# A ring of three weight halves, and edge rows gathered plainly and summed by VectorE

## The reference

```python
feat = jnp.concatenate([n_f[edge_src], n_f[edge_dst]], axis=1)
e_oo = jax.nn.relu(feat[E_HH:E_HH + E_OO] @ W_oo + b_oo)
logit = (e_f @ W_a + b_a)[:, 0]
m = jax.lax.stop_gradient(jax.ops.segment_max(logit, edge_dst, num_segments=N))
ex = jnp.exp(logit - m[edge_dst])
alpha = ex / den[edge_dst]
z_f = jax.ops.segment_sum(alpha[:, None] * n_f[edge_src], edge_dst, num_segments=N)
h_new = jax.nn.relu(nf2[:NH] @ W_hn + b_hn)
```

## Time and profile before

| | |
|---|---|
| median of three runs | 787.23 us (786.36 to 787.28) |
| the profiled execution | 785.15 us, its span 783.4 us |
| PE busy | 660.7 us (84% of the span) |
| DVE busy | 505.2 us (64%) |
| POOL busy | 259.7 us (33%) |
| ACT busy | 209.5 us (27%) |
| DMA packets of the gathers' queue | 20160, 73.41 MB, 36.1% of 16 engines' span |
| DMA packets of SP's queue | 20800, 88.88 MB, 30.1% |

### The profile page before, as it was taken

How to read it: one execution, slowest core, us unless ns; L and a number is a source line. 1 busy time by engine, 2 the same in 40 slices (tenths; PEclk the granted TensorE clock), 3 DMA queues, 4 the chain that set the end, 5 groups by cost and what they waited for, 6 DMA issues and landing times. The chain is left out here.

```text
span 783.4 us, 8227 instructions
## 1 busy us (share of the span) xinstructions
PE 660.7 (84%) x2739; PEld 467.8 (60%) x2741; DVE 505.2 (64%) x1084; ACT 209.5 (27%) x266; POOL 259.7 (33%) x191
## 2 busy tenths in 40 slices
PE   4999999999847997798999699999955676798952
PEld 3778887788735775575778456677710011586621
DVE  8968813635645556365764597865568896327996
ACT  4333322220332354041614425152220100311001
POOL 3000306655654206247475555401223000002340
PEclk9999999999988999798999999999995779899985
DMA  9753449999999768969999999945360023140201
GB/s 347 257 203 135 141 184 298 296 323 320 323 303 317 269 200 226 306 200 312 306 287 296 317 318 236 303 151 189 108 242 0 0 80 135 54 140 5 108 27 80
DMA packets 41721, 163.40 MB, mean 209 GB/s; under 512 B 5168, under 2 KB 5552, under 8 KB 34512
## 3 DMA queue, kind: packets, MB, share of 16 engines
q0 software_dynamic: 20160, 73.41, 36.1%
q1 hardware_dynamic: 20800, 88.88, 30.1%
q10 hardware_dynamic: 720, 0.59, 0.2%
HBM read 146.08 MB, written 16.78 MB: 208 GB/s over the span
## 5 line engine op out<-in xcount | busy, mean ns | idle before, releaser
L1384 PE MATMUL bank_low<-w_hi,xT_hi 128*128 128x512 f32 x496 | 201.7, 407 | 8.2 <-DVE w_lo L861 3.2
L1385 PE MATMUL bank_low<-w_lo,xT_hi 128*128 128x512 f32 x496 | 196.4, 396 | 0.0
L1386 PE MATMUL bank_low<-w_hi,xT_lo 128*128 128x512 f32 x496 | 196.2, 396 | 0.0
L560 POOL DMA_INDIRECT gathered_rows<-edge_tables,dst_row x68 | 115.8, 1703 | 76.8 <-DMA gathered_rows<-edge_tables,src_row 65.5
L1029 DVE SCALAR_TENSOR_TENSOR gathered_rows<-gathered_rows,wa_bc 128x1024 f32<-128x1024 f32 x68 | 83.0, 1221 | 83.1 <-DMA gathered_rows<-edge_tables,dst_row 83.1
L560 POOL DMA_INDIRECT gathered_rows<-edge_tables,src_row x68 | 87.0, 1279 | 127.2 <-DVE gathered_rows L1029 91.8
L861 DVE TENSOR_TENSOR w_lo<-w_raw,w_hi 128x2048 fp32r<-128x2048 f32 x48 | 107.9, 2288 | 31.2 <-ACT w_hi L633 30.9
L1384 PEld LDWEIGHTS bank_low<-w_hi,xT_hi 128*128 128x128 f32 x496 | 95.3, 192 | 38.0 <-issue 12.3
L1386 PEld LDWEIGHTS bank_low<-w_hi,xT_lo 128*128 128x128 f32 x496 | 95.0, 191 | 20.6
L1385 PEld LDWEIGHTS bank_low<-w_lo,xT_hi 128*128 128x128 f32 x496 | 95.2, 192 | 18.7
L633 ACT ACTIVATE w_hi<-w_raw 128x2048 fp32r<-128x2048 f32 x50 | 92.8, 1902 | 8.3 <-DMA w_raw<-in_wt 8.3
(11 more groups left out here) (269 smaller groups left out, 951.7 us busy)
## 6 DMA issues: line engine op xcount, KB each, us to landing
w_raw<-in_wt SPq DMA_DIRECT2D x54, 1024.0 KB, 8.2
edge_tables<-stage SPq DMA_DIRECT2D x32, 256.0 KB, 7.1
x_in<-in_x SPq DMA_DIRECT2D x4, 512.0 KB, 9.1
xn_scratch<-xn SPq DMA_DIRECT2D x4, 512.0 KB, 4.6
node_top<-stage SPq DMA_DIRECT2D x8, 256.0 KB, 7.7
x_part<-in_x SPq DMA_DIRECT2D x8, 256.0 KB, 5.5
mix_out<-stage SPq DMA_DIRECT2D x8, 256.0 KB, 2.0
xn_raw<-xn_scratch SPq DMA_DIRECT2D x4, 512.0 KB, 5.8
```

The costliest lines, as they stand in the source:

```text
L560: pool.indirect_dma_start(rows_sum[:, s, :], None, table_d[0:rows, :], bass.IndirectOffsetOnAxis(ap=index[:, t:t + 1].bitcast(U32), axis=0 ...
L1384: pe.matmul(dest, lh, rh, start=start and i == 0, stop=False)
L1385: pe.matmul(dest, lh, rl, start=False, stop=False)
L1386: last = pe.matmul(dest, ll, rh, start=False, stop=last_one)
```

## The change

- **Ring.** `w_hi` and `w_lo` hold three halves each instead of two chunks. PE goes through the first half for all row blocks, then through the second, with one bank per row block. A new semaphore `first_halves` tells ACT that a chunk's first half has been read, upon which the second half of the next chunk is copied. SP, ACT and DVE take halves one at a time (`load_next`, `hi_half`, `lo_half`). The very last half, BON1's second, has a place of its own.
- **Edge rows.** With the space that this frees there are five src and five dst buffers in place of six slots. Both gathers of a tile are plain and are issued one behind the other. DVE adds the two (L1052, 128x1024) before the dot. That is 68 more DVE instructions.
- **Order.** Tiles no longer come in pairs: `TILES` says how many stand behind a chunk's first and second half on DVE, and a tile's maximum is taken one tile later. The k and q sums stand in one row behind the chunk's tiles. `ATTEND`, `DEN8` and `KV_AT` move PE's small products to other places. All 36 maxima stand in PR1.

The diff, cut to its core:

```diff
-PAIRS = {4: 2, 5: 3, 6: 2, 7: 3, HHT0: 1, HHT1: 1, K0: 3, V0: 3, HN1: 1, K1: 3, V1: 3, Q0: 2, Q1: 3, ON0: 3, ON1: 1}
-assert sum(PAIRS.values()) * 2 == T_GATHERED
-MAXIMA = {PR0: (0, 18), PR1: (18, 36)}
+RING = 3
+TILES = {5: (3, 2), 6: (3, 2), 7: (3, 2), HHT0: (1, 2), HHB0: (1, 1), HHT1: (1, 2), HHB1: (1, 1),
+         K0: (3, 2), HN0: (1, 1), V0: (2, 3), HN1: (0, 1), K1: (2, 3), V1: (2, 3), Q0: (2, 3), Q1: (2, 3),
+         ON0: (2, 2), ON1: (2, 2), PR0: (2, 0)}
+assert sum(map(sum, TILES.values())) == T_GATHERED
+MAXIMA = {PR1: (0, 36)}
 T_EARLY = 36
-SLOTS = 6
+SLOTS = 5
+LAG = 2
+SECOND = 5
 LOADED = 4
+ADDED_HERE = list(range(T_GATHERED))
...
-USES = [("k", a, j) for a in range(2) for j in range(4)] + [("q", 0, j) for j in range(4)] + \
-       [("q", 1, 0), ("q", 1, 1), ("q", 1, 2), ("z", 0, 0), ("z", 0, 1), ("q", 1, 3), ("z", 0, 2), ("z", 0, 3)] + \
-       [("z", 1, j) for j in range(4)]
-
-ATTEND = {(Q1, 2): [(0, 0), (0, 1)], (Q1, 3): [(0, 2), (0, 3)], (ON0, 2): [(1, 0), (1, 1)], (ON1, 0): [(1, 2)], (ON1, 1): [(1, 3)]}
-DEN8 = {(Q1, 0): 0, (ON0, 0): 1}
+USES = [("k", a, j) for a in range(2) for j in range(4)] + [("q", 0, j) for j in range(4)] + [("z", 0, j) for j in range(4)] + \
+       [("q", 1, j) for j in range(4)] + [("z", 1, j) for j in range(4)]
+
+ATTEND = {(Q1, 1, 0): [(0, 0), (0, 1)], (Q1, 1, 1): [(0, 2), (0, 3)], (ON0, 1, 0): [(1, 0), (1, 1)], (ON0, 1, 2): [(1, 2), (1, 3)]}
+DEN8 = {(Q1, 0, 2): 0, (ON0, 0, 1): 1}
+KV_AT = {(HN1, 0, 0): 0, (Q0, 0, 0): 1}
...
+    w_hi = sb("w_hi", [P, RING, HALF], F32R, at_w_hi)
     bhn1 = sb("bhn1", [P, 2, HALF], F32, at_w_hi)
-    w_lo = sb("w_lo", [P, 2, KT * CW], F32R)
+    w_lo = sb("w_lo", [P, RING, HALF], F32R)
...
+        def load_next(c, h):
+            sp.wait_ge(w_lo_done, 2 * (c - 1) + h + 1)
+            load_half(c, h)
+            if h == 0 and c in BIASED:
+                sp.wait_ge(bias_lo_done, bias_no(c))
+                load_bias(bias_no(c))
+
         for c in range(TABLES):
-            for h in range(2):
-                sp.wait_ge(w_lo_done, 2 * (c + 1) + h + 1)
-                load_half(c + 2, h)
-            if c + 2 in BIASED:
-                sp.wait_ge(bias_lo_done, bias_no(c + 2))
-                load_bias(bias_no(c + 2))
+            load_next(c + 2, 0)
             for m in range(MT):
                 store(4 * c + m + 1, m % 2, table_tiles[c // 2, m, :, (c % 2) * CW:(c % 2 + 1) * CW])
+            load_next(c + 2, 1)
...
+                s = t % SLOTS
                 if t >= SLOTS:
                     pool.wait_ge(edge_dot, t + 1 - SLOTS)
-                gather(t, src_row, src_landed)
-            if t >= LAG:
-                u = t - LAG
-                pool.wait_ge(src_landed[u % SLOTS], 16 * (u // SLOTS + 1))
-                gather(u, dst_row, dst_added, ALU.add)
+                gather(t, rows[:, s, :], src_row, src_landed[s])
+                if t in ADDED_HERE:
+                    n = ADDED_HERE.index(t)
+                    if n >= SECOND:
+                        pool.wait_ge(row_added_here, n + 1 - SECOND)
+                    gather(t, dst_rows[:, n % SECOND, :], dst_row, dst_landed[s])
...
+        def hi_half(c, h):
+
+            if h == 0:
+                act.wait_ge(prod_ready, FIRST[c - 1] + HEAD)
+                if c in BIASED:
+                    n = bias_no(c)
+                    act.wait_ge(bias_loaded, n * 32 + 32)
+                    act.activation(b_hl[0:64, n % 2, :], b_raw[0:64, :], ACT.Copy).then_inc(bias_hi_done, 1)
+            elif c == BON1:
+                act.wait_ge(prod_ready, FIRST[BON0] + HEAD)
+            else:
+                act.wait_ge(first_halves, c)
+            act.wait_ge(raw_loaded[h], 16 * (c + 1))
+            act.activation(w_half(c, h)[0], raw[:, h, :], ACT.Copy).then_inc(w_hi_done, 1)
...
+        def edge_tile(t):
 
             if t % LOADED == 0:
+                catch_up()
                 load_blocks(t)
-            for u in range(2):
-                s = (t + u) % SLOTS
-                mask_others(t + u)
-                dve.wait_ge(dst_added[s], 16 * ((t + u) // SLOTS + 1))
-                dve.scalar_tensor_tensor(out=rows_sum[:, s, :], in0=rows_sum[:, s, :], scalar=0.0, in1=wa_bc[:, :], op0=ALU.max, op1=ALU.mult,
-                                         accum_out=logit[:, t + u:t + u + 1]).then_inc(edge_dot, 1)
-            for u in range(2):
-                dve.wait_ge(edge_dot, t + u + 1)
-                take_max(t + u)
+            s, landed = t % SLOTS, 16 * (t // SLOTS + 1)
+            mask_others(t)
+            row = rows[:, s, :]
+            if t in ADDED_HERE:
+                n = ADDED_HERE.index(t)
+                dve.wait_ge(src_landed[s], landed)
+                dve.wait_ge(dst_landed[s], landed)
+                dve.tensor_tensor(row, row, dst_rows[:, n % SECOND, :], ALU.add).then_inc(row_added_here, 1)
+                catch_up()
+                dve.wait_ge(row_added_here, n + 1)
+            else:
+                catch_up()
+                dve.wait_ge(dst_landed[s], landed)
+            dve.scalar_tensor_tensor(out=row, in0=row, scalar=0.0, in1=wa_bc[:, :], op0=ALU.max, op1=ALU.mult,
+                                     accum_out=logit[:, t:t + 1]).then_inc(edge_dot, 1)
+            behind.append(t)
...
         for c in range(TABLES, PR1 + 1):
-            split_chunk(c + 1)
-            work = []
             if c == HHT0:
                 split_feat(1)
-            if c in (HHB0, HHB1):
-                work = [lambda i=i, half=int(c == HHB1): hh_logits(half, i) for i in range(2)]
+            lo_half(c, 1)
             if c == K0:
                 finish_hh()
 
                 dve.memset(kvb[:, :, :], 0.0).then_inc(kv_cleared, 1)
                 dve.memset(vbuf[:, :, :, P:P + 1], 1.0).then_inc(kv_cleared, 1)
-            if c in (K0, K1):
-                work = [lambda j=j, a=int(c == K1): add_kq("k", a, j) for j in range(4)]
             if c == K1:
                 spread_ks(0)
+            edge_work(c, 0)
             if c == Q0:
                 spread_ks(1)
-                work = [lambda j=j: add_kq("q", 0, j) for j in range(4)]
-            if c == Q1:
-                work = [lambda: add_kq("q", 1, 0), lambda: invert_den(0), lambda: add_kq("q", 1, 1), lambda: add_kq("q", 1, 2),
-                        lambda: attend(0, 0), lambda: attend(0, 1), lambda: add_kq("q", 1, 3), lambda: attend(0, 2), lambda: attend(0, 3)]
-            if c == ON0:
-                work = [lambda: invert_den(1), lambda: attend(1, 0), lambda: attend(1, 1)]
-            if c == ON1:
-                work = [lambda: attend(1, 2), lambda: attend(1, 3)]
-            edge_work(c, work)
+            if c in (Q1, ON0):
+                a = int(c == ON0)
+                invert_den(a)
+            lo_half(c + 1, 0)
+            if c in (Q1, ON0):
+                for j in range(4):
+                    attend(int(c == ON0), j)
+            edge_work(c, 1)
+            if c in (HHB0, HHB1):
+                for i in range(2):
+                    hh_logits(int(c == HHB1), i)
+            if c in (K0, K1):
+                for j in range(4):
+                    add_kq("k", int(c == K1), j)
+            if c in (Q0, Q1):
+                for j in range(4):
+                    add_kq("q", int(c == Q1), j)
+            if c == PR0:
+                catch_up()
             if c in MAXIMA:
                 take_maxima(*MAXIMA[c])
+        lo_half(BON0, 1)
...
+        def chunk_product(c, lhs, before=None):
+
+            for h in range(2):
+                pe.wait_ge(w_lo_done, 2 * c + h + 1)
+                for i, m in enumerate(ROWS[c]):
+                    b = bank_of[c, i]
+                    if h == 0:
+                        free(c, i)
+                        if c in BIASED:
+                            pe.wait_ge(bias_lo_done, bias_no(c) + 1)
+                            add_bias(b, c, True, False)
+                    if c in (Q0, Q1):
+                        last = half_product_q(b, c, h, i)
+                    else:
+                        last = half_product(b, c, h, m, lhs, h == 0 and c not in BIASED and c not in (HHB0, HHB1),
+                                            h == 1 and c not in (HHT0, HHT1), before if i == 0 else None)
+                    if h:
+                        last.then_inc(prod_ready, 1)
+                    elif i == len(ROWS[c]) - 1:
+                        last.then_inc(first_halves, 1)
+                    if (c, h, i) in KV_AT:
+                        kv_product(KV_AT[c, h, i])
+                    if (c, h, i) in DEN8:
+                        den8(DEN8[c, h, i])
+                    for a, j in ATTEND.get((c, h, i), ()):
+                        attend(a, j)
```

(30 more changed lines are left out.)

241 lines of the change are left out of this document (102 added, 139 removed).

## The result

| | before | after |
|---|---|---|
| median of 12 runs each | 786.98 us (784.38 to 789.66) | 790.38 us |
| ratio after/before | | 1.0038, 95% interval 1.0020 to 1.0057 |
| profiled execution, its span | 785.15, 783.4 us | 789.31, 787.5 us |
| DVE busy | 505.2 us | 581.7 us |
| PE starts V0 | 316.67 us | 305.7 us |

The changed kernel is slower by a little more than the measurement leaves open. The forecast was 789.5 us. Eleven of the twelve runs lie between 784.87 and 792.16 us, with a median of 789.93; the twelfth took 1102 us at a granted clock of 0.56 and counts in the 790.38, but not in the ratio.

A forecast was written before the change was run, and what follows sets the result against it. Gather to gather to DVE to PE bounds the kernel; afterwards DVE ends the stretch. V0 at 310.6 plus 264 us returns DVE at 574.6 against 572.2: 785.15 + 2.4 = 787.5 profiled, 789.5 forecast with 2.1 for the median, range 774 to 806.

The forecast's parts named there:

- The bound: Up to DVE's return at the exponents: DVE takes PE's place as what ends the stretch; 574.6 us against PE's 561.
- its last sign: After DVE's return at the exponents: forecast wrong if this part, 213 us before, changes by more than 2 us.
- The additions: DVE's edge tiles: 68 additions at 1.14 us, 77.5 us of DVE work, making a tile 3.25 us.
- Stretch A: End of chunk 7 to V0: 102 us with DVE setting it, V0 at 310.6 us, 16.6 us earlier.
- Its two waits: DVE between chunk 7 and V0: 5.8 us for the low features, 3.5 us before the four k sums.
- the early gain of 16.6 us: At V0's start: 310.6 us instead of 327.2, then spent by DVE's additions before its return.
- Stretch B: V0 to DVE's return at the exponents: 232 us of DVE work plus 31.6 of waits, 264 us.
- the wait ahead of the maxima: DVE before PR1's 36 maxima: 12.3 us waiting for BON0's half, behind x loads, POOL's addition, stores and ACT.
- The removed waits: DVE before the dots of edge tiles: 83.1 us of waits for rows gone, one landing instead of two.
- The first: Up to DVE's return: waits overlap, PE stays the bound and ends at 561; 777 us, faster, chance 0.32.
- The second: Edge tiles: the gathers set the pace, 3.7 us per tile instead of 3.25; 801 us, slower, chance 0.14.
- The third: PE's long stalls before DVE's work stay, early gain 6 instead of 16.6 us; 800 us, slower, chance 0.11.

The follow-up runs named there:

- the split run: The changed kernel with the maxima split as before, 18 in PR0 and 18 in PR1: 781.39 us, ratio 0.9917 to the kernel before.

## Why the prediction was right

**The bound.** It named DVE's queue as what would end the stretch, with PE done earlier. Both are so: PE ended PR1 at 567.8 us (561 forecast), DVE returned at 579.5 (574.6 forecast). Of the signs that the prediction named, a tile at 3.2 to 3.3 us, no long wait for landings, PE idle before the maxima end and the wait for the exponents gone came out. V0 at 308 to 313 (305.7) and DVE back at 572 to 578 (579.5) did not, and by its last sign the forecast was wrong: the part after DVE's return changed by 3.2 us, more than the 2 that it allowed.

**The additions.** 68 at 1.219 us; the 37 tiles from V0 on cost 121.6 us, 3.29 each, against 3.25. The price of the work was right. The prediction never put a price on it in time; the runs give 34 us against none at all, 24 us in the kernel before, and 13 to 14 us against adding in flight.

**Stretch A.** The sum for DVE's own work, 92.8 us, holds (eight half logits and k sums at 0.7 are 5.6 and not 5.4): from 208.2 to V0 the changed kernel's DVE was busy for 85.9 and read block numbers for 4.6. Its two waits were 9.3 in the forecast. Of the 5.8 us for the low features 2.7 were lost behind the end of chunk 7 (207.3), since DVE had stood 8 of its 10.94 us for them before. The waits for ACT before the k sums were 2.2 instead of 3.5. V0 came at 305.7 instead of 310.6.
One number of this step was read wrongly. I took 327.2 us as the start of V0 before. The row at 316.67 us of the earlier trace rows is already V0's first bias, and 327.2 is its second row block. The gain up to V0 was therefore 11.0 us and not 21.5, and of the forecast 16.6 us 10.5 were never there. It does not enter the sum for DVE, which goes by the absolute times 310.6 and 574.6, but "the early gain of 16.6 us" was in truth one of 6 in my own count. It does enter PE's time. The 231.3 us of work after V0 leave out V0's first row block, 9.0 us of work from that row to this one of the kernel before:

```profile
327.16 0.50 PE L1392 MATMUL bank_low<-b_hl,ones_b 64*128 64x512 f32 x1
```

With it PE's end of PR1 would have been forecast at 570 instead of 561, some 5 us ahead of DVE instead of 13.6, and PE's 92 us of work in stretch A were 9 too many. PE worked 244.3 us from V0 on and stood 17.8 (19 forecast), and ended at 567.8.

**Stretch B.** 264 us forecast, 273.8 measured. The work came out as priced but for the attends: eight took 23.9 us with their waits for ACT, against 16. The largest term was undersized: the wait ahead of the maxima was 16.8 us, not 12.3. The chain was the right one, but its first link took 11.9 us, from SP's first load of x at 532.49 to POOL's addition at 544.42, and not the 5.5 of one load. The loads alone explain less: where POOL did wait for x, in PR1 of the split run, it began 7.8 us after the first of the four. What is left fits POOL's reduction. The profile shows 1.80 or 3.88 us for it, and yet POOL's next instruction began 11.1 to 12.0 us after its start in the changed kernel and in the eleven runs made from it. That POOL is busy all that time is inferred, and was not tested by a run of its own. The 20.54 us of the earlier trace rows were no sign of it: there the reduction had begun at 520.69, the loads of x at 534.09, and the last of them did release POOL.
Errors of 5 us early and 10 us late partly cancelled, and 3 us more went back behind DVE's return: it took 210 us to the end instead of 213. All 3 lie in the hot rows, from DVE's return to PE's first work on their result (93.1 us instead of 96.1, and 94.0 to 95.5 in five of the variants); their cause stays open. So the mechanism was right, but that 787.5 was forecast for the profiled execution and 789.3 measured is closer than the steps deserve, and part of it is luck.

**The removed waits.** "DVE's 83.1 us of waits for rows as gone" was exact. My explanation of them was half wrong. I said two landings one after the other; ten slots with a longer lag left 51 of 57 us of them, and each landing took longer. The same 73.41 MB cost the DMA engines 36.1% of 783.4 us, 283 us, when the second gather added in flight, and 25.8% of 787.5 us, 203 us, when both were plain. It is 80 us of all sixteen engines, in a stretch where they were full, that the plain gathers save. With DVE free of additions this was worth 20 us (756.05 against 776.22); with them, DVE's queue took its place.

**The rivals.** The first (PE ends it, 777) did not come about, and its 561 for PE rested on the misread start of V0. With the maxima split PE was done at 563.3, DVE still came back 5.9 us behind it, after ACT's copy of the last half and its own, and the time was 781.4. The second (the gathers set the pace) did not show at all. The issues were slow, with a median of 1.84 us for a src gather and 1.21 for a dst gather, and 0.94 for both with the additions cut to one column, but no DVE instruction waited for a row. That fits the rule of the Trainium skill, "SBUF — State Buffer", "Who interferes with whom", on two SBUF inputs only as far as POOL is concerned, and only if the issue of a gather reads SBUF, which no run here shows: POOL's instruction lengthened, while DVE's additions took their 1.22 us throughout.
The third (the stalls stay) was partly right: of 15.1, 9.1 and 7.7 us there remain 2.1, 9.3 and 6.5.

## What to carry to other kernels

A wait in the queue of an in-order engine is not free time: of 77 us of work put where 83 us of waits stood, 24 came out at the end of the kernel. Before exchanging a transfer's work for an engine's, ask which of the two has slack in that stretch; here the DMA engines were full and it still paid to leave the additions to them, since DVE sat on PE's path. And when a long block of independent work (the 36 maxima) can stand on either side of a wait, put it in front of it: that alone was worth 7 to 8.5 us by the medians and 4 to 5.5 in the traces, more than the difference that the whole change made.

## What the runs showed of the hardware

- A gather of 128 rows of 4 KB that adds in flight takes the DMA engines longer than a plain one. The packets of the gathers' queue took 203 us of all sixteen engines with 136 plain gathers, so 101 for 68, and 283 us with 68 plain and 68 adding ones, so 182 for the 68 that add: 1.8 times as much, by this estimate. With 34 adding ones it was 246 us (31.7% of 776.5), halfway. The queue's few other packets are counted as gathers.
- The reduction over the partitions of 128x512 on POOL is shown with 1.80 or 3.88 us, and POOL's next instruction began 11.1 to 12.0 us after its start in twelve traces.
- The reading of four block numbers on DVE leaves a gap of 1.54 to 2.05 us beside the gathers, 24.4 us for 15 of them, and 1.27 to 1.55 us ahead of the maxima in PR1.
- More gathers in flight did not land more rows in the same time: with rows added in flight, six slots had a median of 12.2 us from issue to landing and ten slots 21.8, at a DMA share of 1.04 to 1.05 in both.
